# GpSimd's split of four weight tiles waits for the complete adjacency matrix, in place of running beside its last groups

## The reference

```python
def sage_conv(x, edge_index, W_l, b_l, W_r):
    msgs = x[src]
    agg = segment_sum(msgs, dst, num_segments=x.shape[0])
    cnt = segment_sum(ones, dst, num_segments=x.shape[0])
    agg = agg / maximum(cnt, 1.0)[:, None]
    return agg @ W_l.T + b_l + x @ W_r.T
h = relu(sage_conv(x, edge_index, W1_l, b1, W1_r))
return sage_conv(h, edge_index, W2_l, b2, W2_r)
```

## Time and profile before

| | |
|---|---|
| median of 3 executions | 1817.26 us (1813.61, 1817.26, 1817.34) |
| the profiled execution, its own time | 1814.99 us |
| its span | 1813.0 us |
| TensorE / VectorE / ScalarE / GpSimd busy | 91% / 62% / 49% / 40% |
| mean granted TensorE clock | 0.962 of full speed |

### The profile page before, as it was taken

The page is one execution under the profiler, slowest core; times in us unless marked ns, Lnnn a source line. Parts: engine busy times, 40 slices in busy tenths (PEclk is TensorE's granted clock), DMA queues, the critical chain, the costliest instruction groups (busy, mean ns, idle before and its releaser), DMA issues.

```text
span 1813.0 us, 27124 instructions
## 1 busy us (share of the span) xinstructions
PE 1651.4 (91%) x9904; PEld 1377.0 (76%) x9904; DVE 1125.9 (62%) x1802; ACT 882.3 (49%) x1728; POOL 727.4 (40%) x593
## 2 busy tenths in 40 slices
PE   2897989849999999987999998999999997899997
PEld 1565876538788888875878998787888886688876
DVE  7895134730488889852038887418988887853332
ACT  3894221322388788722217776207878784401100
POOL 3122020034734465032356873544544458532431
PEclk9998999969999999988999999999999998899999
DMA  3000000131212111033122230421112120011111
GB/s 106 8 24 24 0 29 12 51 143 36 57 30 57 30 30 41 12 93 141 36 57 58 58 70 7 166 63 30 29 30 57 36 81 18 20 33 41 41 40 56
DMA packets 33000, 88.40 MB, mean 49 GB/s; under 512 B 5190, under 2 KB 5660, under 8 KB 32369
## 3 DMA queue, kind: packets, MB, share of 16 engines
q1 hardware_dynamic: 32881, 86.83, 17.5%
HBM read 43.29 MB, written 12.80 MB: 31 GB/s over the span
## 4 chain that ended last, share of the span: by engine, by line
PE 75%; DVE 8%; ACT 5%; POOL 4%; DMA 3%; issue 3%; SPq 1%; DVEq 1%; POOLq 0%; ACTq 0%
PE ps L686 12%; PE ps L907 12%; PE ps L687 11%; PE ps L688 11%; PE ps L888 11%; PE ps L873 7%; PE ps L874 6%; PE ps L813 2%; DMA w_raw<-in_weights 2%; PE ps L814 1%; PE ps L923 1%; POOL F L603 1%; ACT F L1082 1%; DVE stats L1303 1%; ACT F L1175 1%
## 5 line engine op out<-in xcount | busy, mean ns | idle before, releaser
L548 POOL TENSOR_TENSOR w_hi<-w_raw,zero 128x512 fp32r<-128x512 f32 x96 | 111.7, 1163 | 712.2 <-PE ps L688 437.0
L1095 ACT ACTIVATE R<-ps 125x500 fp32r<-125x500 f32 (+3 forms) x632 | 291.2, 508 | 147.3 <-PE ps L888 145.8
L1547 DVE TENSOR_REDUCE TB<-ps 125x1 f32<-125x1250 f32 (+4 forms) x240 | 299.5, 1262 | 82.6 <-PE ps L874 56.1
L1556 DVE TENSOR_TENSOR R<-ps,R 125x500 fp32r<-125x500 f32 (+3 forms) x632 | 323.8, 568 | 10.9 <-ACT R L1095 10.9
L1082 ACT ACTIVATE F<-ps,TB 125x1250 f32<-125x1250 f32 (+4 forms) x240 | 276.0, 1157 | 88.6 <-DVE TB L1547 88.6
L907 PE MATMUL ps<-R 125*128 125x252 f32 (+1 forms) x2080 | 288.9, 286 | 2.3 <-DVE F L1599 2.3
L888 PE MATMUL ps<-ident,F 125*125 125x125 f32 x2040 | 259.3, 275 | 8.3 <-ACT F L1082 7.3
L907 PEld LDWEIGHTS ps<-R 125*128 125x128 f32 x2080 | 255.9, 189 | 2.6 <-DVE R L1556 1.6
L888 PEld LDWEIGHTS ps<-ident,F 125*125 125x125 f32 x2040 | 239.1, 189 | 11.6 <-ACT F L1082 11.3
L873 PE MATMUL ps<-R 128*125 128x512 f32 (+5 forms) x624 | 240.0, 385 | 5.1 <-DVE R L1556 3.9
L686 PE MATMUL ps<-R,w_hi 128*128 128x512 f32 (+1 forms) x576 | 209.9, 364 | 38.0 <-POOL w_lo L563 14.0
(11 more groups left out here) (175 smaller groups left out, 2459.0 us busy)
## 6 DMA issues: line engine op xcount, KB each, us to landing
R<-F SPq DMA_DIRECT2D x96, 312.5 KB, 5.2
w_raw<-in_weights SPq DMA_DIRECT2D x96, 256.0 KB, 2.6
TB<-in_x SPq DMA_DIRECT2D x10, 250.0 KB
x_d<-F SPq DMA_DIRECT2D x10, 250.0 KB
zt_d<-F SPq DMA_DIRECT2D x1, 2500.0 KB, 10.2
F<-zt_d SPq DMA_DIRECT2D x1, 2500.0 KB, 12.9
xt_d<-F SPq DMA_DIRECT2D x4, 625.0 KB, 3.6
qc_d<-F SPq DMA_DIRECT2D x4, 625.0 KB, 2.9
```

The costliest lines, as they stand in the source:

```text
L548: return eng.tensor_tensor(to, a, zero[0:to.shape[0], :].to_broadcast(list(to.shape)), ALU.add)
L1095: eng.activation(probs_run(K, n, 0, part, lo, hi), ps[0:P, 3 * (n % 2) + bank, P * (lo - j0):P * (hi - j0)] .rearrange("p (c t) -> p c t", ...
L1547: ins = eng.tensor_reduce(out=ngm[0:P, 2 * (n % 2) + part:2 * (n % 2) + part + 1], in_=flat(n % 2)[0:P, at:at + P * blocks], op=ALU.max, a ...
L1556: eng.tensor_tensor(probs_run(K, n, 1, part, lo, hi), ps[0:P, 3 * (n % 2) + bank, P * (lo - j0):P * (hi - j0)] .rearrange("p (c t) -> p c ...
```

## The change

The unit list is cut at 8. GpSimd splits units 4 to 7 as before, waits until all 83 groups are added to `AT`, and then goes on with unit 8. No instruction is added to or taken from another engine.

```diff
@@ -660,7 +660,9 @@
             cut_units(0, 4)
             eng.wait_ge(ln0.tr, NT + 2)
             eng.memset(F[0:P, 0:5120], 0.0).then_inc(at_zero, 1)
-            cut_units(4, UNIT["us"])
+            cut_units(4, 8)
+            eng.wait_ge(at_added, NG)
+            cut_units(8, UNIT["us"])
             unit_r()
             cut_heads(KS_)
             cut_units(UNIT["us"] + ahead(KS_), UNIT["ut"])
```

## The result

The changed kernel takes 1810.24 us in the median of 20 executions (1806.38 to 1816.99), the kernel before 1814.32 us in 20 of its own beside it (1810.57 to 1817.34). The ratio is 0.998, with a 95% interval of 0.9971 to 0.9989, so it is faster by 2.0 to 5.3 us, 4.1 at the middle. (The median of 1817.26 us that stood ahead came from three executions; with 20 it is 1814.32.)

A forecast was written before the change was run, and what follows sets the result against it. VectorE's one-hot comparisons, stretched by GpSimd's splits, were taken to bound this stretch. Removing the stretch gives 4.94 us, other terms nothing; from bases giving 1811.2 and 1812.3 it took 1811.6 us, range 1808.5 to 1815.0 (8 in 10).

The forecast's parts named there:

- VectorE's last rounds: Groups 78 to 80: three rounds of about 2.6 us, stretched by GpSimd's splits, return to 0.96, saving 4.94 us.
- What would be late next: TensorE's and ScalarE's work for the last groups is done in time, so the whole 4.94 us reaches the last add.
- The lower bound of 4.6: Gain in us that remains at the last add if TensorE's last group were late by 0.3 us.
- The passage to the aggregate: From last add to ScalarE's L1146 stays 2.28 us; all behind it follows, so 4.94 us pass to the end.
- GpSimd at its new place: Moved splits, from about 154.9, are done by 165.5, before VectorE's next instruction at 166.2: no overlap.
- The slower rival: Splits hold up the aggregate's start by up to 10 us; at full price 5 us slower, 1821; chance 0.03.
- The clock: TensorE restarts the aggregate at half clock as before, worth nothing; bounds 2.5 us gained to about 1 us lost.
- The rival of a clock that stays up: TensorE starts the aggregate at full clock: 7.4 us gained in all, 1808.7 to 1809.9; chance 0.08.
- The rival of a gain too small to tell: Whole kernel: a price of 1.3 us or more leaves the gain under about 0.2%, 1813.7 to 1816; chance 0.17.
- the edge that the prediction drew: For the whole kernel, about 0.2% (3.6 us) is what a measurement can tell from no change.

The follow-up runs named there:

- e1: Changed kernel plus eight GpSimd instructions at the old place, of the splits' kind and size, reading w_raw; 1815.32 us, ratio to before 1.0008.
- e3: Changed kernel with the wait in front of unit 10 instead of 8, so units 8 and 9 split at the old place; 1813.70 us, ratio 0.999.
- e5: Changed kernel plus 24 GpSimd memsets at the old place, which write SBUF and read nothing; 1810.97 us, ratio 0.9977.
- e9: Changed kernel plus filler matmuls on TensorE before eight slow restarts, 50 of them before the temporal queries; 1814.45 us, ratio 0.9992.
- e7: Changed kernel plus 16 filler matmuls on TensorE behind the last group, before the first aggregate; 1808.70 us, ratio 0.9966.
- e11: Changed kernel with SP's ten stores of the intermediate x each issued after its tile, not behind all loads; 1798.91 us, ratio 0.9910.

## Why the prediction was right

1. *VectorE's last rounds, 4.94 us.* Measured 4.93. Rounds of 0.96 us in place of 2.6; e1 brings the old value back with instructions that do nothing else, e3 half of it. Right in place, size and cause. The cause had rested on agreement of the earlier trace rows with the Trainium skill; e5 shows that it is not GpSimd's being busy, and fits the Trainium skill's rule that it is its reading.
2. *What would be late next: nothing.* The adds fell where the step put them, counted from the eviction, and TensorE's last group started at 151.83, 1.25 us before the last add. The lower bound of 4.6 was not needed.
3. *The passage to the aggregate, 2.28 us from the add's end to L1146.* Now 155.72 - 153.45 = 2.27. The step said that nothing behind it has a clock of its own. That held for this change, as SP's first store moved with the rest (353.04 to 346.70 us), but it was said too broadly: in e9 3.5 us were swallowed by the train of stores, whose length is their own and not the aggregate's. The prediction had not looked at what the router waits for.
4. *GpSimd at its new place, free.* Done at 163.27 (165.5 expected, from a start 1.4 us later), before VectorE's instruction of 164.86; ScalarE's roundings took 1.35 us. The slower rival, splits that hold up the aggregate, fell by this row.
5. *The clock, worth nothing in the difference.* A slow restart again, 5.2 us at 0.51. The rival of a clock that stays up did not come. Its size, 2.5 us, was right: e7 measured 2.35. On the rule of the Trainium skill ("TensorE: Matmul & The Clock Gate", Part 1), that idleness lowers the clock and activity brings it back, the row at 156.59 and e7's at 156.39 agree: 0.76 us behind an idle gap of 4.25 us, 0.47 us behind the fillers.
6. *The number.* 1811.6 forecast, 1810.24 measured, within 1808.5 to 1815.0. That it came so near is in part luck, for two errors work against each other. The base was 2.2 us too high: 1811.6 stands for a kernel before of 1811.6 + 4.94 = 1816.5, from four executions, and twenty gave 1814.32. The gain in the medians was 4.1 us and not 4.94, which takes back 0.9. Against the base of twenty the shift of 4.94 would give 1809.4, and the interval of 2.0 to 5.3 us holds it. The profiled pair's 7.5 us would have misled, had it been read as the gain. The rival of a gain too small to tell came close: the ratio of 0.998 lies on the edge that the prediction drew, by the spread of the times and not by a step that failed.

## What to carry to other kernels

An instruction of GpSimd that reads SBUF beside VectorE instructions with two SBUF inputs costs VectorE about 0.8 us a collision here; where VectorE sets the pace, move GpSimd's work by one wait to a place where VectorE is idle or reads PSUM, and compare the durations of one line in the two surroundings to find such places. Measure an effect of a few microseconds inside one execution, between two events close on both sides, for whole executions lie up to 7 and 11 us apart (before and after). And look ahead for the next thing on another queue that a gain has to pass: here ten stores queued behind loads were worth more than twice the change.

## What the runs showed that was not expected

- Fifty fillers in e9 stood where TensorE has no gap and cost 11 us; the loss was in their place, not in the clock. Before placing a filler, read that the engine is idle at this point of its program.
- Ten stores of 250 KB, issued back to back, took 24.3 us in one execution and 27.6 in another (first issue to the router's step), and kept the router waiting for 11.83 and 15.15 us.
- The order in which two engines first collide (36 to 51 us) moved VectorE's first comparison by 3 us between executions of kernels that are the same up to there (51.18 us in the changed kernel, 54.96 in e11).
